# Own product first, next split second: the order of ACT and DVE in a shared-expert step

## The reference, cut to what matters

```
shared = silu(x @ sh_gate_w.T) * (x @ sh_up_w.T) @ sh_down_w.T        # I_SH = 1408
for e in range(8):                                                    # top 2 of 8 experts a token
    cur = silu(gate) * up @ down_proj[e].T                            # I_MOE = 352
    out = out + cur * combine[:, e:e+1]
out = out + sigmoid(x @ shared_gate_w.T) * shared
x = x + layernorm(out)
```

## Time and profile before

| | |
|---|---|
| median of 3 runs | 2139.0 us (2136.22 to 2146.01) |
| profiled execution | 2138.97 us, its span 2136.5 us |
| PE busy | 1983.1 us, 93% of the span |
| DVE, ACT, POOL busy | 1485.9, 1164.0, 748.4 us |
| experts phase | from about 1446 us to the end |
| mean granted TensorE clock | 0.973 of full |

### The profile page before, as it was taken

One profiled execution on the slowest core, in us unless ns is written; L12 is line 12 of the kernel. 1 busy time (PEld: TensorE's weight loads), 2 busy tenths in 40 slices (PEclk: granted clock), 3 DMA queues, 4 the chain that ended last, 5 costly groups with the idle time before them and its releaser, 6 DMA issues. The chain is left out here.

```text
span 2136.5 us, 32819 instructions
## 1 busy us (share of the span) xinstructions
PE 1983.1 (93%) x10142; PEld 1667.6 (78%) x10142; DVE 1485.9 (70%) x3511; ACT 1164.0 (54%) x2946; POOL 748.4 (35%) x1058
## 2 busy tenths in 40 slices
PE   7999999759999999999999999868999999999996
PEld 6677787537888888888888888756878888888775
DVE  7788547657766776767767777884467887774664
ACT  6742222336666666666666666643367776673332
POOL 3441001345555555555555555640600000001442
PEclk9999999869999999999999999978999999999998
DMA  7431110262000000000000000122689898884553
GB/s 253 137 130 51 42 36 20 99 243 96 21 11 21 10 0 30 0 20 10 20 10 20 10 1 6 65 69 87 239 315 327 315 322 309 306 307 156 170 187 109
DMA packets 82292, 244.78 MB, mean 115 GB/s; under 512 B 10464, under 2 KB 11104, under 8 KB 80256
## 3 DMA queue, kind: packets, MB, share of 16 engines
q1 hardware_dynamic: 77040, 226.46, 30.7%
q0 software_dynamic: 5120, 16.78, 2.3%
HBM read 207.81 MB, written 45.61 MB: 119 GB/s over the span
## 5 line engine op out<-in xcount | busy, mean ns | idle before, releaser
L269 PE MATMUL att_ps_xt<-att_w_hi,xT_hi 128*128 128x512 f32 x512 | 206.6, 404 | 28.2 <-DVE att_w_lo L2541 12.4
L2484 POOL TENSOR_SCALAR att_pr<-att_pr,att_ri 128x384 f32<-128x384 f32 (+2 forms) x256 | 136.5, 546 | 271.4 <-DVE att_ri L2579 271.4
L269 PE MATMUL att_ps_xt<-att_w_hi,xT_lo 128*128 128x512 f32 x512 | 204.5, 399 | 0.0
L269 PE MATMUL att_ps_xt<-att_w_lo,xT_hi 128*128 128x512 f32 x512 | 204.3, 399 | 0.0
L2677 ACT ACTIVATE att_pr<-att_pr,att_nb,att_r 128x384 f32<-128x384 f32 (+2 forms) x256 | 168.0, 659 | 36.8 <-DVE att_nb L2566 36.2
L2622 ACT ACTIVATE att_qkv<-att_ps_xt 128x512 f32<-128x512 f32 x128 | 76.3, 596 | 201.2 <-PE att_ps_xt L269 192.8
L1826 POOL DMA_INDIRECT y<-moe_rows,moe_slotA x16 | 16.0, 999 | 415.0 <-DMA moe_rows<-moe_lo_f 411.9
L2669 ACT ACTIVATE att_pT_hi<-att_ps_pt 128x768 fp32r<-128x768 f32 (+2 forms) x128 | 93.7, 732 | 122.7 <-PE att_ps_e L269 120.7
L269 PEld LDWEIGHTS att_ps_xt<-att_w_hi,xT_hi 128*128 128x128 f32 x512 | 97.6, 191 | 58.8 <-POOL att_w_lo L2457 23.2
L2489 POOL TENSOR_TENSOR att_rot<-att_rot 128x384 f32<-128x384 f32 x128 | 129.2, 1009 | 17.5 <-DVE att_rot L2532 17.5
L2549 DVE TENSOR_TENSOR att_q_lo<-att_ps_xt,att_q_hi 128x256 fp32r<-128x256 f32 x128 | 54.1, 423 | 112.9 <-ACT att_k_hi L2659 112.9
(11 more groups left out here) (329 smaller groups left out, 6682.6 us busy)
## 6 DMA issues: line engine op xcount, KB each, us to landing
y<-in_moe_rt SPq DMA_DIRECT2D x59, 704.0 KB, 6.5
y<-in_moe_rt SPq DMA_DIRECT2D x39, 768.0 KB, 6.5
moe_sraw_gu<-in_moe_sgu SPq DMA_DIRECT2D x44, 512.0 KB, 3.9
moe_sraw_d<-in_moe_sd SPq DMA_DIRECT2D x44, 256.0 KB, 4.2
moe_xs<-in_zeros SPq DMA_DIRECT2D x39, 256.0 KB, 9.4
moe_lo_f<-moe_xs SPq DMA_DIRECT2D x39, 256.0 KB, 6.7
moe_rows<-moe_lo_f SPq DMA_DIRECT2D x39, 256.0 KB, 6.6
att_raw_w<-in_qkv_w SPq DMA_DIRECT2D x8, 1024.0 KB, 4.8
```

Source lines behind the costliest of these rows:

```text
L269: mm = pe.matmul(out, lhsT, rhs, start=(i == 0), stop=(i == len(terms) - 1))
L2484: pool.tensor_scalar(p, p, ri[:, j % 2, g:g + 1], 1.0, ALU.mult, ALU.mult).then_inc(s("p"), 1)
```

## The change

Within a shared step, ACT and DVE do `sd_split(n)` and the step's own SiLU or product first, and only then `sgu_split(n + 1)`; the split of `hs` follows as before. Nothing is added or removed. SP, POOL and PE keep their programs.

```diff
@@ DVE @@
                 if kind == "S" and n < N_SH:
+                    sd_split(n)
+                    s_mul(n)
                     if n + 1 < N_SH:
                         sgu_split(n + 1)
-                    sd_split(n)
-                    s_mul(n)
                     hs_split(n)
@@ ACT @@
                     if n % SH_CHUNKS == 1 and n > 1:
                         shared_out(n // SH_CHUNKS - 1)
+                    sd_split(n)
+                    s_silu(n)
                     if n + 1 < N_SH:
                         sgu_split(n + 1)
-                    sd_split(n)
-                    s_silu(n)
```

## The result

The changed kernel takes 2171.3 us in the median (2167.04 to 2177.55, four runs), the kernel before 2139.2 beside it. The ratio is 1.0151 with a 95% interval of [1.0124, 1.0178]: about 32 us slower. The profiled execution took 2170.13 us with a span of 2167.6, so 31.1 us more of span than before. I had forecast 2152, and no more than 2164. The direction and its mechanism are as forecast, the size is not. Two executions of the whole study, one of the kernel before (3286 us at a mean granted clock of 0.56) and one of old_order_behind_tile (2501 us, 0.74), were in a slow state and stand in no ratio.

A forecast was written before the change was run, and what follows sets the result against it. PE was taken to bound the experts phase. Against the profiled 2138.97 us, +1.0 + 1.2 - 0.4 + 17 + 0.4 - 6 gave +13.2, so 2152 us, range 2136 to 2164.

The forecast's parts named there:

- Step 0: First shared step: no down matmuls cover the later split, so gate 1 starts at 1472.0; cost 1.0 us.
- The load loop: Steps 4 to 10: down weights behind SiLU and split make the loop outlast the step; +1.2 us, bounds 0.3 and 3.
- S 11 and the first tile: Entry to routed stretch: a 0.91 us gate wait goes, tile loads leave a split later; -0.4 us, bounds -0.9 and +1.
- The routed stretch: Twelve cycles: loads leave 5.7 us later, token tiles land late, 1.5 us a cycle; +17 us, bounds 5 and 25.
- the fixed 2.5 us: Routed stretch: part of a tile's landing time taken as constant, added to its bytes at 355 GB/s.
- The tail: Late shared steps: most stalls from late gate and up weights go; -6 us, bounds -11 and 0.
- The rule on DVE and POOL: Tail: a two-SBUF-input DVE operation and a GpSimd operation reading SBUF exclude each other; a split met took 1.54 us over usual.
- the worst case: Tail: all 13 splits met in full by POOL's addition would give 12 us back, cancelling the gain.
- The queue absorbs the late load: Rival, routed stretch: tiles land within 11.2 us of the late load's issue, cost 5 or less; 2140 us, chance 0.25.
- 91% share: Routed stretch: DMA engines 91% busy over 300 us, used as an argument against the late load being absorbed.
- Hidden loads and a freed tail: Rival: routed cost 0, tail -11; 2130 us, or 2126 with old tile waits gone; chance 0.10.
- The tail keeps its stalls: Rival: down weights or POOL's addition replace the late weights, tail 0, queue starves; 2158 us, up to 2166; chance 0.17.

The follow-up runs named there:

- old_order_behind_tile: Kernel before, old order everywhere, with SP issuing the shared loads of steps 11 to 23 behind the next routed tile's: ratio 0.9993, -1.5 us.
- routed_only: Kernel before with the new order in steps 11 to 24 alone, on both ACT and DVE: ratio 1.0127, +27.2 us.
- late_by_silu: Kernel before, with SP's gate and up load in steps 11 to 23 waiting for the step's SiLU, 1.6 us later: ratio 1.0011, +2.4 us.
- loads_behind_tile: Changed kernel, with SP issuing the shared loads of steps 11 to 23 behind the next routed tile's loads: ratio 1.0015, +3.2 us against before.

## Why the prediction was right in kind and wrong in size

The reading of the bound, the direction and the place of the largest term held: PE waits for token tiles behind a load that leaves 5.7 us later. It was 18 us short (2152 against 2170.1 in the profiled execution). By its own steps:

- **Step 0**, +1.0 forecast: PE waited 0.91 us for the split and gate 1 came 0.97 late. Right. Not foreseen: gate 1's own matmuls then ran at a granted clock of 0.66 (1470 to 1475), and gates 1 to 4 lost 2.1 us more. PE's timeline parts the two causes. Between gates 1 and 2, 1.5 us are lost with no wait of PE; eight matmuls there start 0.42 us apart, where 0.23 is usual, and 8 x 0.19 is that 1.5:

```profile
1471.86 0.63 PE L269 MATMUL moe_ps_g<-xT_hi,moe_sgu_hi 128*128 128x512 f32 x1
1472.28 0.63 PE L269 MATMUL moe_ps_g<-xT_lo,moe_sgu_hi 128*128 128x512 f32 x1
```

  That is the clock. Of the 0.5 us between gates 2 and 3, 0.36 are a wait for the split, behind a SiLU that late down weights held up (ACT waited 3.98 us for them).
- **The load loop**, +1.2: +1.5 between gates 4 and 10. Right in total; four of the six steps are 8.7 to 8.9 us long and two keep 8.39.
- **"S 11 and the first tile", -0.4: the step that failed.** I wrote that "the tile loads behind the held load leave a split later" and gave that nothing. What is left of a step's slack by then I never worked out for step 10, whose held load stands ahead of tile 0. There the tile's load left 1.9 us later and landed 1.8 later, PE waited 5.35 us, and the turn at 1588.60 another 4.08. Gates 10 to 12 lost 8.8 us, the largest miss of the sum. One half is tied to step 10 by an experiment (3.9 us). The other, 4.8 between gates 11 and 12, is the first case of the cycle's loss. In routed_only, where the front keeps the old order, the same two gates lost 2.7; why it is more in the changed kernel, and more than in later cycles, wasn't tried.
- **The routed stretch**, +17, bounds 5 and 25: +23.2 over the twelve cycles. The waits there are 19.8 us, where the kernel before has 1.7: +18.1, so the total was sized well, but not by a right model. I had 0.5 us a cycle for the first tile behind a step and 1.0 for the second; it is 1.5 on the first (18.5 us in eleven waits), and the second is late once in twelve. The rate up to the landing, 348 GB/s, is near the 355 that I took, but not the bytes, and the fixed 2.5 us is no fixed time. The first bytes move about 1.0 us behind the issue. Until the tile landed, 4.39 MB moved, of which only 3,200 KB (3.28 MB) were issued ahead of it or with it: the other 1.1 MB, 3.2 us at 348 GB/s, belong to transfers issued behind it (the store of rows and the next pairs are the first of them). With 9.4 us for the 3.28 MB, 1.0 + 9.4 + 3.2 gives 13.6 us; it took 13.5. The tile does not have the DMA engines to itself because it was issued first. By the Trainium skill (DMA: Bandwidth & Descriptors, Two DMAs through the same engine are not ordered) nothing orders transfers across the 16 engines; the 4.39 MB agree, though they don't show which engine was behind. And later the rate was 411, not 355, which fits the second tile's being in time.
- **The clock** was no term of the sum. Behind two of the twelve waits PE's clock fell towards its lower level of 1.2 GHz:

```profile
1652.00:1656.00 4.00, 3.74 (x12) 3.13 (x13) 2.06 (x2) 1.98 (x2) 0.00 (x0) 0.57 1.03 416
1808.00:1812.00 4.00, 3.78 (x14) 2.97 (x15) 2.29 (x3) 1.97 (x2) 0.00 (x0) 0.68 1.02 418
```

  With 1812 to 1816 (0.90) that is 3.4 us of full clock, two thirds of the 5.1 that the twelve cycles lost beyond their waits; at the entry, 1584 to 1596, it is 3.4 again. What the last 1.7 are isn't shown.
- **The tail**, -6: -5.0 in the traces, -3.4 when tried alone. The mechanism held, no wait for `hs` is left. The rule on DVE and POOL that I weighed, from the Trainium skill (SBUF — State Buffer, Who interferes with whom), bears out in part: the split of 2083.27 takes 1.21 us over the usual while POOL's addition takes 1.30. Of the 13 tail splits from 2029 on eight are 1.75 us or longer. One line of the view by tile, 2040 to 2145, gives least, median and longest in ns:

```profile
L1944 DVE TENSOR_TENSOR moe_sgu_lo<-moe_sraw_gu,moe_sgu_hi x12: 1208/1872/2431, 2038.4 to 2138.1; 128x1024 fp32r<-128x1024 f32 x12
```

  PE's waits for the split in the tail are 4.8 us, not the 12 of the worst case.
- **The rivals.** "The queue absorbs the late load" was to hold if the tile landed within 11.2 us of the late load's issue. It took 13.5 (1671.14 to 1684.6). late_by_silu shows the same rival true for a load that is 1.6 us later. My argument against it, "91% share", was no argument: loads_behind_tile moved nearly the same bytes at a share of 0.81, with PE busy for 299.8 of 300 us. "Hidden loads and a freed tail" needed a routed cost of 0 and is out at 23.2; "The tail keeps its stalls" is out at -5.0.

## What to carry to other kernels

A load that waits for a buffer holds everything behind it on its queue: before moving the work that frees the buffer, list what stands behind the load and when each of these is due, the transitions between phases too. If there is anything due sooner, issue that first and the held load behind it; here that turned +32 us into +3, and with the new order kept out of the front into -6. Give a late stream its slack and, as a first guess, a price of one for one behind it, and add a term for the clock where waits of 2 us come again and again.

## What the runs showed of the hardware

- The clock does not fall behind each stall. Of waits of about 2 us, those that ended at 1652.26 (1.97 us) and 1808.22 (1.95) were followed by a granted clock of 0.57 and 0.68; those that ended at 1684.59 (2.04) and 1899.16 (2.36) were not. So a stall of 2 us has no fixed price. A shorter one was followed by a fall too: behind 16 small matmuls and a wait of 0.91 us that ended at 1470.20, the clock was 0.66 over the next 5 us. In the kernel before, with the same matmuls and no such wait, it stayed full.
- An issue can cost SP far more than its usual 0.33 to 0.43 us. Of the tile loads and stores of rows between 1600 and 1930, 18 of 64 took over 0.6 us in the changed kernel (up to 1.76; the store at 1675.41 took 1.38), and 4 of 69 in the kernel before (up to 1.04). The 113 issues of pairs and routed down weights in that stretch of the changed kernel took 0.33 to 0.52 each. What makes an issue slow isn't shown.
- The same bytes can be moved at very different shares: 317 GB/s at 0.91, and 313 GB/s at 0.81 in loads_behind_tile.
